# Large attention of a perceiver block: the scores for the row maximum from 64 rows of keys in two halves of the array, instead of from 128 rows

## The chip, the cores and the metric

The kernel runs as one program on one core of a Trainium2 chip (trn2). The metric is the time of one execution on the device in microseconds (us). The core has five engines that run side by side: TensorE (PE in the profile, its weight loads as PEld), VectorE (DVE), ScalarE (ACT), GpSimd (POOL) and SyncE (SP), which here only starts DMA transfers. They wait for one another by semaphores.

## What is computed

Two blocks of a perceiver, six sublayers with residuals, on x of shape (32, 64, 256) and a context of shape (32, 1601, 64). The change lies in the fourth sublayer, the large attention over the context, 16 heads:

```python
q_hk = (hidden_q @ Wq.T).reshape(Bv, Sv, H, K)
q_big = jnp.einsum('bshk,hkq->bshq', q_hk, w_kc_q)
q_big = _apply_rope(q_big, sin_q[None, :, None, :], cos_q[None, :, None, :])
kv_r = _apply_rope(kv_c, sin_k[None], cos_k[None])
q_r = jnp.einsum('bshq,hqr->bhsr', q_big, W_qr)
k_r = jnp.einsum('bld,hdr->bhlr', kv_r, W_kr)
scores = jnp.einsum('bhsr,bhlr->bhsl', q_r, k_r)
attn = jax.nn.softmax(scores, axis=-1)
ctx_c = jnp.einsum('bhsl,bld->bhsd', attn, kv_r)
ctx_lat = jnp.einsum('bhsd,hkd->bhsk', ctx_c, w_kc_kv)
```

In the kernel the products with the weights of queries and keys are merged, so that the scores are products of 64-element effective queries with the turned context.

## The kernel before

The phases run one after the other: three small attentions and two MLPs stand around the large attention (`context_attention`), which takes about 742 to 2519 us of the profiled execution. A batch there is one of the 32 sequences: 16 heads x 64 queries (1024 columns of queries) against 1601 keys in 13 tiles of 128 (the last has 65).

Numbers are kept as two parts in a reduced format (F32R), a high part and the rest. `kp` holds a batch's turned keys: the high parts in rows 0 to 63, the low parts in rows 64 to 127. `q1` holds the high parts of the queries in both halves of the rows. SyncE copies `kp` into `k1` and the high rows into `k2` (`move`), once a batch; `k2` and `q2` carry the rest of the product and the negated maximum in one further row.

For each tile kt of a batch n TensorE runs three thirds: `scores` for the first and for the second half of the heads (two 512-column products each, L813 and L814), and `values` (L825), which multiplies the exponentials that ScalarE made of an earlier tile. `values` writes to 64 of the 128 output rows at a time, so its products are 128 by 64 in the array, the others 128 by 128. GpSimd adds the exponentials up (L685).

The softmax needs each row's maximum ahead of the exponentials. So while batch n goes through its tiles, the maximum of batch n+1 is made in 16 pieces (`max_scores`, L790). A piece takes 128 query columns as weights and streams half of the keys as two products of 402 keys, into the two banks of one of the two `mx` buffers; VectorE reduces both banks in one instruction (`reduce_max`, L1062). Piece i waits for the reduction of piece i - 2. `pieces` sets where they stand: in an even batch (e = 0) from the second third of tile 1 to the second third of tile 6, in an odd one from tile 3 to tile 9, at most one behind each third. By that rule an even batch has 5 pieces behind the first scores of a tile, 6 behind the second scores and 5 behind the values; an odd batch has 6, 5 and 5. The 16 pieces of batch 0 stand side by side ahead of the first batch. Even batches also make the queries of the next two batches (L747, L761) in tiles 7 to 11.

The keys of batch n+2 are turned by TensorE in tiles 7 to 10 of batch n (L728) and kept in `kp` by ScalarE one tile later (L924).

Of the kernel before, what the change touches and what calls it, by code (L numbers as in the profile page):

```python
# [8 lines left out]
F32 = mybir.dt.float32  # L9
F32R = mybir.dt.float32r  # L10
# [5 lines left out]
P = 128  # L16
# [9 lines left out]
DCX = 64  # L26
# [375 lines left out]
SKP = 1608  # L402
KQ = SKP // 4
NKT = -(-SK // P)
SKT = NKT * P
KROUNDS = 4
# [75 lines left out]
def context_attention(nc, sb, pb, sem, a, x_all, const, wbig, mw, wvo):  # L482
# [16 lines left out]
    kr = sb("cx_kr", [P, NKT, DCX])  # L499
    khl = sb("cx_khl", [P, NKT, 2, DCX])  # L500
    kp = [sb(f"cx_kp{i}", [P, SKT], F32R) for i in range(2)]
    k1 = [sb(f"cx_k1{i}", [P, SKP], F32R) for i in range(2)]
    k2 = [sb(f"cx_k2{i}", [P, SKP], F32R) for i in range(2)]
    kv = [sb(f"cx_kv{i}", [P, NKT, DCX]) for i in range(2)]
# [21 lines left out]
    mx = [pb(f"cx_mx{i}", [P, 2, 512]) for i in range(2)]  # L526
# [13 lines left out]
    s_kl = sem("cx_kl_kept")  # L540
    s_kt = sem("cx_keys_transposed")
    s_kp = sem("cx_turned_keys_kept")
    s_kd = [sem("cx_even_keys_moved"), sem("cx_odd_keys_moved")]
    s_kv = sem("cx_kv_kept")
    s_var = sem("cx_variance")
# [53 lines left out]
    def batches(engine, before, batch):  # L599


        before()
        batch(0, 0, 0, True, True, True)
        with engine.Fori(0, NT - 2) as t:
            batch(2 * t + 1, t, 1, True, True, True)
            batch(2 * t + 2, t + 1, 0, True, True, True)
        batch(B - 3, NT - 2, 1, True, True, False)
        batch(B - 2, NT - 1, 0, False, True, False)
        batch(B - 1, NT - 1, 1, False, False, False)

    def is_first(n):
        return isinstance(n, int) and n == 0

    with nc.Block() as block:

        @block.sync
        def _(sp):
            def fetch(n):
                sp.dma_start(ctx[:, :, :], a["cx_ctxN"][bass.ds(n, 1), :, :, :]).then_inc(s_ctx, 16)
                sp.dma_start(ctxr[:, :, :], a["cx_ctxrN"][bass.ds(n, 1), :, :, :]).then_inc(s_ctx, 16)  # L620

            def move(n, e):

                sp.wait_ge(s_kp, KROUNDS * (n + 1))
                if not isinstance(n, int) or n >= 2:

                    sp.wait_ge(s_st, (n - 1) * 2 * NKT)
                sp.dma_start(k1[e][:, :].bitcast(F32), kp[e][:, 0:SKP].bitcast(F32)).then_inc(s_kd[e], 16)
                sp.dma_start(k2[e][0:DCX, :].bitcast(F32), kp[e][0:DCX, 0:SKP].bitcast(F32)).then_inc(s_kd[e], 16)

            def before():
                fetch(0)
                sp.wait_ge(s_kr, 1)
                fetch(1)
                sp.wait_ge(s_set, 6)
                move(0, 0)
                sp.wait_ge(s_kr, 2)
                fetch(2)

            def batch(n, t, e, more, next, far):  # L640
                if next:
                    move(n + 1, 1 - e)
                if far:

                    sp.wait_ge(s_kr, n + 3)
                    fetch(n + 3)

            batches(sp, before, batch)

        @block.gpsimd  # L650
# [69 lines left out]
        def _(pe):  # L720
# [52 lines left out]
            def max_scores(t, n, e, i):  # L773
                b = i % 2
                if i == 0:

                    pe.wait_ge(s_kp, KROUNDS * (n + 1))
                    if e == 0:
                        pe.wait_ge(s_q1a, 2 * t + 2)
                        pe.wait_ge(s_q2a, 2 * t + 2)  # L780
                    else:
                        pe.wait_ge(s_q1b, t + 1)
                        pe.wait_ge(s_q2b, t + 1)
                if not (is_first(n) and i < 2):

                    pe.wait_ge(s_mr, n * PIECES + max(i - 1, 0))
                q = q1[e][:, :, :, :].rearrange("p e j s -> p (e j s)")[:, (i // 2) * P:(i // 2 + 1) * P]
                for h in range(2):
                    lo = (2 * b + h) * KQ
                    last = pe.matmul(mx[b][:, h, 0:KQ], q, kp[e][:, lo:lo + KQ], start=True, stop=True)  # L790
                last.then_inc(s_mx, 1)

            def max_rows(n, p):
# [54 lines left out]
            def before():  # L848
                pe.wait_ge(s_set, 6)
                pe.wait_ge(s_one, 1)  # L850
                for r in range(KROUNDS):
                    turn_keys(0, r)
                turn_x(0)
                for j in range(CP + 2):
                    queries(0, j)
                for i in range(PIECES):
                    max_scores(0, 0, 0, i)
                for r in range(KROUNDS):
                    turn_keys(1, r)
                max_rows(0, 0)  # L860
                max_rows(0, 1)
                scores(0, 0, 0, 0, 0)
                scores(0, 0, 0, 0, 1)
# [1026 lines left out]
```

## Time and profile before

| | us |
|---|---|
| median of the three timed runs | 3383.43 |
| lowest and highest of them | 3383.25 and 3397.73 |
| the profiled execution | 3396.48 |
| its span, first to last instruction | 3394.7 |
| TensorE busy in the span | 2916.8 (86%) |
| VectorE, ScalarE, GpSimd busy | 1579.7, 1260.5, 1232.9 |

The profile is of one execution. Times in it are microseconds from the start of the span unless marked ns. An engine is busy while it computes; the ends of matmuls are modelled, since they are pipelined, so durations of two neighbours overlap, and the distance of two starts tells what one really takes.

### The profile page before, as it was taken

Reading aid. Unit: us, or ns where it says so; the run is one execution under the profiler, and the core shown is the slowest. Engines: PE = TensorE matmul, PEld = TensorE weight load, DVE = VectorE, ACT = ScalarE, POOL = GpSimd, SP = SyncE. Lnnn points to the kernel's source line nnn. Section 1 sums busy time; section 2 is a strip of 40 time slices with the busy share of each in tenths; the row PEclk is TensorE's granted clock in tenths of the full one; section 3 lists DMA queues with packets and bytes.
Section 4 is the critical chain, followed back from the end, with each engine's and each line's share of the span. In section 5 each row is a group of like instructions: output and inputs, shape, how many; then the busy total and the mean of one; then the engine's idle time right before and its main releaser. Section 6 shows DMA issues by size and latency. Waiting matters only on the chain. (4 is left out here: it accounts for less than half of the span.)

```text
span 3394.7 us, 49700 instructions
## 1 busy us (share of the span) xinstructions
PE 2916.8 (86%) x17527; PEld 1787.8 (53%) x17528; DVE 1579.7 (47%) x2705; ACT 1260.5 (37%) x2514; POOL 1232.9 (36%) x656
## 2 busy tenths in 40 slices
PE   5867734659999999999999999999977789999998
PEld 3544422535545554555455554555434467777776
DVE  3444567533554455444544464445526643333232
ACT  3433412114344334433443344344424333333332
POOL 0000000035676567656765676557650000000000
PEclk9778866679999999999999999999988899999999
DMA  1000030011111011110111111111011000000000
GB/s 40 0 17 0 0 121 0 0 58 40 36 49 39 25 35 49 39 35 33 41 39 35 39 35 39 35 39 35 30 72 77 0 1 0 0 0 0 0 0 25
DMA packets 26434, 98.27 MB, mean 29 GB/s; under 512 B 3536, under 2 KB 8272, under 8 KB 24976
## 3 DMA queue, kind: packets, MB, share of 16 engines
q1 hardware_dynamic: 24720, 94.02, 8.4%
q10 hardware_dynamic: 1664, 3.58, 0.3%
q8 instruction: 32, 0.52, 0.1%
q14 instruction: 18, 0.15, 0.0%
HBM read 55.97 MB, written 2.10 MB: 17 GB/s over the span
## 5 line engine op out<-in xcount | busy, mean ns | idle before, releaser
L685 POOL TENSOR_TENSOR cx_acc<-cx_acc,cx_prob 128x1024 f32<-128x1024 f32 (+1 forms) x352 | 834.7, 2371 | 509.0 <-ACT cx_prob L965 501.5
L965 ACT ACTIVATE cx_prob<-cx_st 128x512 f32<-128x512 f32 (+1 forms) x832 | 477.5, 596 | 595.2 <-PE cx_st L814 577.5
L1062 DVE TENSOR_REDUCE cx_mhalf<-cx_mx 128x1 f32<-128x804 f32 x512 | 486.1, 988 | 219.2 <-PE cx_mx L790 219.1
L825 PE MATMUL cx_av<-cx_prob,cx_kv 128*64 128x512 f32 (+1 forms) x1664 | 456.8, 628 | 0.0
L813 PE MATMUL cx_st<-cx_q,cx_k 128*128 128x512 f32 (+1 forms) x832 | 369.0, 444 | 50.0 <-ACT cx_prob L965 49.4
L1528 PE MATMUL moe_gu<-moe_wgu,moe_xnT 128*128 128x352 f32 x1280 | 397.6, 462 | 0.0
L790 PE MATMUL cx_mx<-cx_kp,cx_q 128*128 128x402 f32 x1024 | 304.0, 380 | 62.6 <-DVE cx_mhalf L1062 59.2
L814 PE MATMUL cx_st<-cx_q,cx_k 128*128 128x512 f32 (+1 forms) x832 | 332.4, 400 | 0.0
L1528 PEld LDWEIGHTS moe_gu<-moe_wgu,moe_xnT 128*128 128x128 f32 x1280 | 241.5, 191 | 124.1 <-issue 6.2
L790 PEld LDWEIGHTS cx_mx<-cx_kp,cx_q 128*128 128x128 f32 x1024 | 174.7, 193 | 248.5 <-DVE cx_mhalf L1062 186.0
L1043 DVE TENSOR_TENSOR cx_turn<-cx_mx,cx_tab 128x384 f32<-128x384 f32 x256 | 130.9, 553 | 358.3 <-PE cx_mx L747 358.3
L1663 DVE SCALAR_TENSOR_TENSOR moe_hid<-moe_silu,moe_coef,moe_gu 128x176 f32<-128x176 f32 x320 | 127.0, 397 | 350.2 <-ACT moe_silu L1591 348.1
L813 PEld LDWEIGHTS cx_st<-cx_q,cx_k 128*128 128x128 f32 (+1 forms) x832 | 157.8, 190 | 204.2 <-ACT cx_prob L965 143.7
L1591 ACT ACTIVATE moe_silu<-moe_gu 128x176 f32<-128x176 f32 x320 | 101.6, 318 | 370.8 <-PE moe_gu L1528 370.8
L1493 POOL TENSOR_TENSOR moe_rstd<-moe_mv,minus_half 128x1 f32<-128x1 f32 x16 | 8.8, 549 | 614.2 <-DVE moe_mv L1628 614.2
L1551 PE MATMUL moe_acc<-moe_wd,moe_hidT 128*128 128x256 f32 (+1 forms) x896 | 216.1, 382 | 0.0
L747 PE MATMUL cx_mx<-cx_xnT,cx_wbig 128*128 128x128 f32 x1536 | 204.7, 283 | 0.5 <-ACT cx_xnT L928 0.5
L761 PE MATMUL cx_mx<-cx_turn,cx_mw 128*64 128x128 f32 (+1 forms) x2048 | 197.0, 296 | 0.0
L747 PEld LDWEIGHTS cx_mx<-cx_xnT,cx_wbig 128*128 128x128 f32 x1536 | 183.2, 192 | 25.0 <-issue 16.5
L924 ACT CAST cx_kp<-cx_misc 128x512 fp32r<-128x512 f32 (+1 forms) x128 | 64.8, 507 | 324.2 <-PE cx_misc L728 324.2
L1551 PEld LDWEIGHTS moe_acc<-moe_wd,moe_hidT 128*128 128x128 f32 (+1 forms) x896 | 160.2, 190 | 21.9 <-issue 5.3
L814 PEld LDWEIGHTS cx_st<-cx_q,cx_k 128*128 128x128 f32 (+1 forms) x832 | 156.8, 188 | 7.5
(209 smaller groups left out, 3701.3 us busy)
## 6 DMA issues: line engine op xcount, KB each, us to landing
cx_k<-cx_kp SPq DMA_DIRECT2D x32, 804.0 KB, 4.0
cx_ctx<-in_cx_ctxN SPq DMA_DIRECT2D x32, 416.0 KB, 3.2
cx_ctxr<-in_cx_ctxrN SPq DMA_DIRECT2D x32, 416.0 KB, 3.9
cx_k<-cx_kp SPq DMA_DIRECT2D x32, 402.0 KB, 5.2
moe_wgu<-in_moe_wgu SPq DMA_DIRECT2D x5, 1408.0 KB, 14.6
moe_wd<-in_moe_wd SPq DMA_DIRECT2D x4, 896.0 KB, 24.6
x_all<-in_x SPq DMA_DIRECT2D x1, 2048.0 KB, 4.2
cx_wq<-in_cx_wq SPq DMA_DIRECT2D x1, 2048.0 KB, 11.8
```

What stands on the lines that cost most here:

```text
L685: pool.tensor_tensor(acc[rows, :, :], sofar, prob[slot(kt)][rows, :, :], ALU.add).then_inc(s_acc, 1)
L747: last = pe.matmul(mx[j % 2][:, 0, tile * P:(tile + 1) * P], wbig[:, c, j, tile * P:(tile + 1) * P], xnT[:, c, :], start=(c == 0), stop=(c ...
L761: last = pe.matmul(mx[j // 4][DCX * e:DCX * e + DCX, 1, at:at + P], mw[rows, j, cs, tile, :], turn[j % 2][rows, cs, tile, :, :], start=(cs ...
L790: last = pe.matmul(mx[b][:, h, 0:KQ], q, kp[e][:, lo:lo + KQ], start=True, stop=True)
L813: pe.matmul(st[p][0:nk(kt), :], k1[e][:, keys], q1[e][:, p, :, :], start=True, stop=False)
L814: pe.matmul(st[p][0:nk(kt), :], k2[e][:, keys], q2[e][:, p, :, :], start=False, stop=True)\
L825: last = pe.matmul(av[DCX * p:DCX * p + DCX, :], kv[e][0:nk(kt), kt, :], prob[slot(kt)][0:nk(kt), p, :], start=(kt == 0), stop=(kt == NKT ...
L965: act.activation(prob[slot(kt)][rows, p, :], st[p][rows, :], ACT.Exp).then_inc(s_exp, 1)
L1043: last = dve.tensor_tensor(turn[j % 2][:, cs, :, :, :], q, tab[:, cs, :, :].unsqueeze(2).broadcast_to([P, 3, 2, S]), ALU.mult)
L1062: dve.tensor_reduce(mhalf[:, i // 2, i % 2:i % 2 + 1], mx[i % 2][:, :, 0:KQ], AX.XY, ALU.max)\
L1528: last = pe.matmul(gu[i][:, 0:2 * FE], xnT[g][:, c, :], wgu[:, e, c, :], start=(c == 0), stop=(c == DC - 1))
L1551: last = pe.matmul(acc[:, 0:D], hidT[q % 2][0:n, k % 4, :], wd[0:n, k, :], start=(k == 0), stop=(k == NFC - 1))
```

## The change

Three edits. The low parts of the keys are left out of the maximum: each of a piece's two products now has 64 rows instead of 128, the first in rows 0 to 63 with `kp`, the second in rows 64 to 127 with a new tile `kh2`. `kh2` gets a second copy of the high parts in its upper rows by a new DMA of SyncE for each batch (`double`), which stands behind the fetch of the context in a batch and ahead of `move` of the next. TensorE's wait in front of the first piece is now for this copy instead of for `kp`. The scores that go into the exponentials are made as before.

```diff
+    kh2 = [sb(f"cx_kh2{i}", [P, SKP], F32R) for i in range(2)]
...
+            def double(n, e):
+
+                sp.wait_ge(s_kp, KROUNDS * (n + 1))
+                sp.dma_start(kh2[e][DCX:P, :].bitcast(F32), kp[e][0:DCX, 0:SKP].bitcast(F32)).then_inc(s_k2[e], 16)
+
             def before():
                 fetch(0)
                 sp.wait_ge(s_kr, 1)
                 fetch(1)
                 sp.wait_ge(s_set, 6)
+                double(0, 0)
                 move(0, 0)
                 sp.wait_ge(s_kr, 2)
                 fetch(2)
+                double(1, 1)
...
                     sp.wait_ge(s_kr, n + 3)
                     fetch(n + 3)
+                if more:
+                    double(n + 2, e)
...
-                    pe.wait_ge(s_kp, KROUNDS * (n + 1))
+                    pe.wait_ge(s_k2[e], 16 * t + 16)
...
-                for h in range(2):
-                    lo = (2 * b + h) * KQ
-                    last = pe.matmul(mx[b][:, h, 0:KQ], q, kp[e][:, lo:lo + KQ], start=True, stop=True)
+                for h, k in enumerate((kp[e], kh2[e])):
+                    lo, rows = (2 * b + h) * KQ, slice(DCX * h, DCX * h + DCX)
+                    last = pe.matmul(mx[b][:, h, 0:KQ], q[rows, :], k[rows, lo:lo + KQ], start=True, stop=True)
```

The order of TensorE's instructions stays as it is. On TensorE, the first pieces of an even batch, before (L813 and L814 are scores, L825 values, L790 the piece):

```order
L813 MATMUL cx_st<-cx_q,cx_k 128x512
L814 MATMUL cx_st<-cx_q,cx_k 128x512
L790 MATMUL cx_mx<-cx_kp,cx_q 128x402 x2
L825 MATMUL cx_av<-cx_prob,cx_kv 64x512 x2
L790 MATMUL cx_mx<-cx_kp,cx_q 128x402 x2
```

And now (L824 and L825 are the scores, L836 the values, L801 the piece; cx_kh is `kh2`):

```order
L824 MATMUL cx_st<-cx_q,cx_k 128x512
L825 MATMUL cx_st<-cx_q,cx_k 128x512
L801 MATMUL cx_mx<-cx_kp,cx_q 128x402
L801 MATMUL cx_mx<-cx_kh,cx_q 128x402
L836 MATMUL cx_av<-cx_prob,cx_kv 64x512 x2
L801 MATMUL cx_mx<-cx_kp,cx_q 128x402
L801 MATMUL cx_mx<-cx_kh,cx_q 128x402
```

Each piece keeps its place, and its second product reads another tile (the sizes are of the outputs, which don't change).

On SyncE, one batch of the loop, before (L628 and L629 are `move`, L619 and L620 `fetch`):

```order
L627 ISA [waits cx_turned_keys_kept]
L628 DMA cx_k<-cx_kp 128x1608 [waits cx_scores]
L629 DMA cx_k<-cx_kp 64x1608
L645 REGISTER_ALU
L619 ISA [waits cx_keys_summed]
L619 DMA cx_ctx<-in_cx_ctxN 128x832
L620 DMA cx_ctxr<-in_cx_ctxrN 128x832
```

And now:

```order
L629 ISA [waits cx_turned_keys_kept]
L630 DMA cx_k<-cx_kp 128x1608 [waits cx_scores]
L631 DMA cx_k<-cx_kp 64x1608
L654 REGISTER_ALU
L621 ISA [waits cx_keys_summed]
L621 DMA cx_ctx<-in_cx_ctxN 128x832
L622 DMA cx_ctxr<-in_cx_ctxrN 128x832
L635 REGISTER_ALU
L636 DMA cx_kh<-cx_kp 64x1608 [waits cx_turned_keys_kept]
```

The new copy stands last in the batch, ahead of the next batch's `move`.

## Rows read from the trace of the kernel before

**Rows 1.** The page's head, its busy table and its clock line (40 slices).

```profile
span 3394.7 us, 49700 instructions
...
PE 2916.8 (86%) x17527; PEld 1787.8 (53%) x17528; DVE 1579.7 (47%) x2705; ACT 1260.5 (37%) x2514; POOL 1232.9 (36%) x656
...
PEclk9778866679999999999999999999988899999999
```

**Rows 2.** Table by stretch (length, busy per engine, granted clock): stage, odd batch, even batch.

```profile
742.00:2519.00 1777.00, 1645.71 (x9025) 921.97 (x9024) 873.84 (x1108) 738.27 (x1341) 1149.21 (x520) 0.98 0.11 36
1501.50:1543.20 41.70, 37.53 (x170) 19.08 (x169) 24.76 (x31) 24.08 (x48) 32.83 (x16) 1.00 0.13 38
1543.20:1611.50 68.30, 64.76 (x406) 38.72 (x405) 31.03 (x41) 22.24 (x38) 39.87 (x18) 1.00 0.11 35
```

**Rows 3.** The page's groups: busy us, mean ns, idle before and its releaser.

```profile
L1062 DVE TENSOR_REDUCE cx_mhalf<-cx_mx 128x1 f32<-128x804 f32 x512 | 486.1, 988 | 219.2 <-PE cx_mx L790 219.1
...
L813 PE MATMUL cx_st<-cx_q,cx_k 128*128 128x512 f32 (+1 forms) x832 | 369.0, 444 | 50.0 <-ACT cx_prob L965 49.4
...
L790 PE MATMUL cx_mx<-cx_kp,cx_q 128*128 128x402 f32 x1024 | 304.0, 380 | 62.6 <-DVE cx_mhalf L1062 59.2
```

**Rows 4.** Timeline of TensorE in an odd batch (start, length, idle before).

```profile
1515.46 0.53 PE L790 MATMUL cx_mx<-cx_kp,cx_q 128*128 128x402 f32 x2
1515.83 0.39 PE L813 MATMUL cx_st<-cx_q,cx_k 128*128 128x512 f32 x1
...
1516.29 0.53 PE L790 MATMUL cx_mx<-cx_kp,cx_q 128*128 128x402 f32 x2
1516.75 1.08 PE L825 MATMUL cx_av<-cx_prob,cx_kv 128*64 128x512 f32 x4
1517.76 0.64 PE L790 MATMUL cx_mx<-cx_kp,cx_q 128*128 128x402 f32 x2
1518.23 0.39 PE L813 MATMUL cx_st<-cx_q,cx_k 128*128 128x512 f32 x1
...
1522.78 0.64 PE L790 MATMUL cx_mx<-cx_kp,cx_q 128*128 128x402 f32 x2 [1.05 <-DVE cx_mhalf L1062]
...
1531.95 0.33 PE L728 MATMUL cx_misc<-ident,cx_khl 128*128 128x128 f32 x1 [0.35 <-POOL cx_khl L668]
```

**Rows 5.** Timeline of TensorE in a small attention, 64 by 64 products (L241).

```profile
2575.47 1.09 PE L241 MATMUL a_score<-a_kbd,a_qT 64*64 64x256 f32 x16
...
2576.50 0.60 PE L235 MATMUL a_score<-maskb,identb 128*128 128x512 bf16 x2
```

**Rows 6.** Timeline of TensorE in the first attention: 128 by 128, 64 by 128, 64 by 64.

```profile
43.41 1.03 PE L194 MATMUL a_front<-a_wq,a_xnT 128*128 128x256 f32 x4
...
44.37 0.70 PE L196 MATMUL a_front<-a_wk,a_ctxT 64*128 64x256 f32 x2
...
45.00 0.65 PE L207 MATMUL a_v<-a_wv,a_ctxT 64*64 64x128 f32 x8
```

**Rows 7.** Timeline of TensorE in an even batch: the pieces that waited longest.

```profile
1560.53 0.63 PE L790 MATMUL cx_mx<-cx_kp,cx_q 128*128 128x402 f32 x2 [0.87 <-DVE cx_mhalf L1062]
...
1565.63 0.64 PE L790 MATMUL cx_mx<-cx_kp,cx_q 128*128 128x402 f32 x2 [1.66 <-DVE cx_mhalf L1062]
```

**Rows 8.** Timeline: last keys kept, first piece after; DMA table: us from issue to landing.

```profile
1541.42 0.27 ACT L924 CAST cx_kp<-cx_misc 128x128 fp32r<-128x128 f32 x1 [0.50 <-PE cx_misc L728]
...
1551.54 0.53 PE L790 MATMUL cx_mx<-cx_kp,cx_q 128*128 128x402 f32 x2
...
cx_k<-cx_kp SPq DMA_DIRECT2D x32, 804.0 KB, 4.0
...
cx_k<-cx_kp SPq DMA_DIRECT2D x32, 402.0 KB, 5.2
```

**Rows 9.** Table by stretch around one fall of the granted clock.

```profile
1620.30:1623.70 3.40, 1.59 (x7) 0.49 (x6) 1.81 (x3) 3.34 (x7) 1.83 (x1) 1.00 0.00 0
1623.70:1627.10 3.40, 3.40 (x9) 1.08 (x8) 0.80 (x1) 1.21 (x3) 3.15 (x2) 0.50 0.00 0
```

More of the change, by code:

```diff
@@ L542, in context_attention @@
     s_kp = sem("cx_turned_keys_kept")
+    s_k2 = [sem("cx_even_kh_doubled"), sem("cx_odd_kh_doubled")]
     s_kd = [sem("cx_even_keys_moved"), sem("cx_odd_keys_moved")]
```

## The prediction

> **What bounds the kernel now.** I read the page's head, its table of engines and its clock line first [rows 1]: TensorE is busy for 86% of the span, and its granted clock stands at nine tenths or more in nearly all slices of the long middle part. The part that the change touches is the context attention, about 742 to 2519 us. The table by stretch gives TensorE 1645.7 of those 1777 us, GpSimd 1149.2, VectorE 873.8, ScalarE 738.3 [rows 2]. So TensorE sets the pace there, and what it loses lies in short waits. The same table for one odd batch (41.7 us wide) and the even batch behind it (68.3 us) leaves TensorE idle for 4.2 and 3.5 us [rows 2]. The groups of the page say what it waits for at the pieces of the maximum: 59.2 us in all, for VectorE's reduction of an earlier piece [rows 3]. VectorE takes 486.1 us of busy time for 512 pieces, 0.95 us each [rows 3], and no piece can start before the reduction that frees its buffer. So there are two regimes: stretches where VectorE paces the pieces, in which time of TensorE is free, and stretches where TensorE works without a gap, in which every tenth of a microsecond counts.
>
> **What the pieces cost now.** In TensorE's timeline I take the time from one group's start to the next group's start, since the ends are modelled. A piece between two scores takes 0.37 us (1515.46 to 1515.83), so one 402-column product takes 0.18 [rows 4]. A piece in front of the values takes 0.46 (1516.29 to 1516.75), and a piece behind them 0.47 (1517.76 to 1518.23) [rows 4]. The values are 128 by 64 products, everything else here is 128 by 128. So each time the shape of the array changes, about 0.10 us goes by before the new shape starts, and its first product is another 0.10 late, since its weights aren't loaded ahead: 0.20 us for a change into a shape with 128 columns.
>
> **Part 1, the products.** One product over 128 rows becomes one over 64 rows, twice, in opposite halves. Two questions decide: do the halves run at once, and does a 64 by 128 shape count as another shape than 128 by 128?
> Halves at once: in the small attention sixteen 64 by 64 products of 256 columns, in both row halves and two banks, take from 2575.47 to 2576.50, 1.03 us [rows 5]. One such pass takes 0.215 us (below), so sixteen in a row would take 3.4 us; they run four at a time. I take this for the new pair, although it has 128 columns and passes once: a piece streams 0.18 us where it streamed 0.37, a gain of 0.18.
> Change of shape: the first attention has just this step. Four 128 by 128 passes of 256 columns take 0.96 us (43.41 to 44.37), which is 0.215 each and 0.10 for leaving; then two 64 by 128 passes take 0.63 (44.37 to 45.00), where 2 x 0.215 is 0.43 [rows 6]. So 64 by 128 pays the full 0.20 us, though only the rows differ.
> Sum by place. A piece between scores and scores adds two changes: 0.40 - 0.18 = +0.22 us. A piece beside the values, or one between values and scores, adds one, since the other is paid already: 0.20 - 0.18 = +0.02. By the kernel's schedule of pieces an even batch has 5 of the first kind and 11 of the second, an odd batch 6 and 10. That is 1.32 and 1.52 us of TensorE time. 16 even and 15 odd batches carry pieces: 21.1 + 22.8 = **44 us**, the upper bound of this part.
> What of it is covered. In the even batch TensorE waits 0.87 us for VectorE before the eighth piece and 1.66 us before the eleventh [rows 7]. The ten pieces that stand ahead of the second wait (three of the dear kind) add 0.80 us, less than the 2.53 of both waits, so it vanishes. Six pieces follow, two of them dear: 0.44 + 0.08 = 0.52, and I take 0.45 because the pieces there are already stretched a little by the same waits. In the odd batch a wait of 1.05 us before the sixth piece swallows what the first five add (0.50), and 0.35 us before the turning of the keys, a wait for GpSimd, swallows a part of the rest [rows 4]. Left are about 1.0 - 0.35 = 0.7 us. 16 x 0.45 + 15 x 0.7 = 7.2 + 10.5 = **18 us**, which is my term. Its lower bound is 0: all of it might fall into waits (TensorE stands for another 49.4 us behind ScalarE's exponentials [rows 3]). The 16 pieces ahead of the first batch are paced by VectorE and stand side by side, so nothing changes there.
> The Trainium skill speaks against the change in the same direction: "TensorEngine Tiling (Array Packing)", Key Properties, says that changing the tiling mode, not merely the tile, drains the engine; its Theoretical Speedup table promises up to 2x for 64 rows. By the table alone a piece would be worth its 0.18 us; the trace agrees with the drain and prices it at 0.20.
>
> **Part 2, the third copy.** SyncE issues one more DMA in every batch, 402 KB, ahead of the two that fetch the keys for the scores. The copy starts when the last round of turned keys is kept (1541.42 + 0.27 = 1541.69) and the first piece that needs it starts at 1551.54, 9.85 us later [rows 8]; on other batches the distance is longer. The existing copy of that size lands 5.2 us after its issue, behind one of 804 KB [rows 8]. So it is hidden, with over 4 us to spare, behind the last scores of the batch and the first two steps of the next. The keys' own copies go about one issue later and aren't needed before the end of the following batch. What queues behind the new wait on SyncE is only the next batch's copy, which waits for the same event or a later one. TensorE's wait for the copy takes the place of the wait for the keys. Cost: 0; if the cover were gone, 16 or 31 times what it is late.
>
> **Part 3, the clock.** The granted clock of TensorE is 0.98 over the stage [rows 2], so about 0.02 x 1777 / 0.5 = 71 us run at the lower of the two levels, 1.2 GHz; part of that is the start of the stage. Where it falls inside, the rows show what came before: 1.59 us busy of 3.4, then 3.4 us at 0.50 [rows 9]. Such a stretch costs at most 1.7 us. The change makes TensorE stream 0.18 us less for each of 16 pieces a batch, and standing still for a change of shape isn't streaming. The even batch's two waits for VectorE [rows 7] become spots as thin as the one in rows 9. Bounds: 0, and a fall in every even batch, 16 x 1.7 = 27 us. I take eight more falls of about 1 us, since part of each lies in a wait: **+8 us**.
>
> **Sum.** 18 + 0 + 8 = 26 us. The profiled execution has a span of 3394.7 us [rows 1] inside 3396.48; it would come to about 3422. The median of the runs is 3383.43, 13 us below the profiled one (one of the timed three was 3397.73), and the same 26 us on it give **3410**.
>
> **Rivals.**
> (a) The added changes of shape fall into waits, and the clock holds: the sum is 0 to 12 us, about 3388. For it: the idle time that TensorE has in both kinds of batch. Against: the six or more pieces behind the last wait.
> (b) Faster: splitting the rows isn't a change of shape for this pair, and weights for one half load while the other works. Then 0.18 us is gained for each piece. VectorE keeps the gain ahead of its waits; behind them 6 pieces in an even batch and 9 in an odd one count (11, less two whose gain the wait of 0.35 us for GpSimd takes): 16 x 6 x 0.18 + 15 x 9 x 0.18 = 17 + 24 = 41 us at most, and I put 35: 3348. It decides as soon as a change costs less than 0.135 us: there are 21 to 22 added changes to 16 pieces, and 0.18 x 16 / 21.5 = 0.135. Against it stands rows 6. In favour is one statement of the Trainium skill, "TensorE: Matmul & The Clock Gate", Part 3 (The mechanism), that weights load beside running products just where the row group differs; in rows 6 it doesn't help, since the step is from all rows to half of them.
> (c) The halves don't run at once in this number format with 128 columns and one pass. Then the 0.18 comes back, on the path for 6 pieces in an even and about 11 in an odd batch: 17 + 30 = 47 us more, and less streaming is then no reason for the clock to fall: 3383 + 18 + 47 = 3448, up to 3383 + 44 + 93 = 3520. Against: rows 5.
> (d) The copy is late. It must take twice what its like takes [rows 8]; 3 us late in every even batch would give 3383 + 26 + 48 = 3457.
>
> **How the numbers follow.** Forecast 0.62 (3396 to 3428), (a) 0.20, (b) 0.06, (c) 0.08, (d) and the rest 0.04. The range takes in (a) and the upper bound of the two terms (44 + 17): 3384 to 3444. About 0.5% (17 us) is what a measurement of this kernel can tell from no change, so slower means over 3400: most of the forecast, all of (c) and (d), 0.66; within 0.5% is (a) and the low end of the forecast, 0.28; faster is (b), 0.06.
>
> **What would show it.** Right: in the timeline the two products of a piece start within 0.01 us of each other; a piece between scores takes about 0.6 us from start to start; the odd batch is longer by 0.7 us, the even one by less; no wait at the first piece for a DMA. Wrong: products 0.18 us apart (c); a piece of 0.2 us with the next scores on time (b); the granted clock of the stage under 0.96 would mean that I put the clock too low.

## The result, and the profile after

The changed kernel takes **3449.12 us** (median of 4 runs, 3441.92 to 3460.75), the kernel before 3384.62 beside it (median of 4, 3383.25 to 3397.73): a ratio of **1.0185, 95% interval 1.0154 to 1.0215**. It is slower, as forecast, but by 64.5 us instead of 26, and 5 us outside the range. The profiled executions differ by the same amount, 3460.75 against 3396.48.

The page's head, its table of engines, its clock line and the groups of the touched lines, of the kernel after (columns as in [rows 1] and [rows 3]):

```profile
span 3459.0 us, 49732 instructions
...
PE 2993.3 (87%) x17527; PEld 1707.7 (49%) x17528; DVE 1592.5 (46%) x2705; ACT 1259.7 (36%) x2514; POOL 1229.2 (36%) x656
...
PEclk9778866669999999999999999999998989999999
...
L1073 DVE TENSOR_REDUCE cx_mhalf<-cx_mx 128x1 f32<-128x804 f32 x512 | 497.1, 991 | 266.9 <-PE cx_mx L801 262.2
...
L824 PE MATMUL cx_st<-cx_q,cx_k 128*128 128x512 f32 (+1 forms) x832 | 405.6, 487 | 49.6 <-ACT cx_prob L976 49.0
...
L801 PE MATMUL cx_mx<-cx_kp,cx_q 64*128 64x402 f32 x512 | 244.5, 478 | 50.9 <-DVE cx_mhalf L1073 47.5
...
L801 PE MATMUL cx_mx<-cx_kh,cx_q 64*128 64x402 f32 x512 | 244.7, 478 | 0.0
```

Against [rows 1] and [rows 3]: the piece is now two groups of 64 by 128 products side by side, 0.478 us each; VectorE's reduction has kept its length (991 ns against 988); TensorE's waits for it have shrunk from 59.2 to 47.5 us; and the other products of TensorE have grown, L824 from 444 to 487 ns in the mean, although nothing was done to them. The clock line looks almost as before. At 40 slices of 86 us it can't show what follows.

The table by stretch, of the kernel after: the stage, one odd batch, and the even batch behind it (length, busy of PE, PEld, DVE, ACT, POOL, granted clock, DMA):

```profile
742.00:2580.00 1838.00, 1715.53 (x9035) 838.14 (x9033) 886.83 (x1109) 741.08 (x1348) 1145.08 (x520) 0.95 0.14 41
...
1534.60:1579.10 44.50, 40.21 (x171) 16.16 (x167) 27.17 (x31) 24.73 (x46) 36.51 (x17) 0.96 0.20 56
1579.10:1650.70 71.60, 68.95 (x413) 37.46 (x415) 29.48 (x40) 22.00 (x41) 35.98 (x16) 0.95 0.12 35
```

The stage has 61 us more than in [rows 2], so nearly all of the loss is in it. From here on a batch is measured from the start of its predecessor's denominators to the start of its own; these are the products that sum up the exponentials (L837, now L848). Without a fall of the clock the kernel before has odd batches of 42.33 us and even ones of 68.2, two such batches of its own by the same table:

```profile
1507.20:1549.50 42.30, 37.77 (x171) 18.94 (x167) 26.77 (x31) 24.68 (x46) 36.62 (x17) 1.00 0.15 49
1549.50:1617.70 68.20, 65.02 (x411) 39.27 (x413) 29.01 (x40) 21.94 (x41) 36.07 (x16) 1.00 0.10 31
```

An odd batch in which the clock falls once takes 43.9 us there. After the change the first of the 14 full odd batches takes 43.0 and the others 44.5, and all 14 full even ones take 71.54 (the first batch of the stage and the last three, which stand without one part or another of the loop, aren't counted).

**Where the 3.3 us of an even batch go.** TensorE's timeline of the kernel after: two scores in a row, a piece between two scores, and the eleventh piece of an even batch:

```profile
1558.00 0.39 PE L825 MATMUL cx_st<-cx_q,cx_k 128*128 128x512 f32 x1
1558.23 0.39 PE L824 MATMUL cx_st<-cx_q,cx_k 128*128 128x512 f32 x1
...
1561.83 0.40 PE L825 MATMUL cx_st<-cx_q,cx_k 128*128 128x512 f32 x1
1562.15 0.44 PE L801 MATMUL cx_mx<-cx_kp,cx_q 64*128 64x402 f32 x1
1562.15 0.44 PE L801 MATMUL cx_mx<-cx_kh,cx_q 64*128 64x402 f32 x1
1562.53 0.51 PE L824 MATMUL cx_st<-cx_q,cx_k 128*128 128x512 f32 x1
1562.87 0.40 PE L825 MATMUL cx_st<-cx_q,cx_k 128*128 128x512 f32 x1
...
1592.64 1.08 PE L836 MATMUL cx_av<-cx_prob,cx_kv 128*64 128x512 f32 x4
1595.27 0.44 PE L801 MATMUL cx_mx<-cx_kp,cx_q 64*128 64x402 f32 x1 [1.55 <-DVE cx_mhalf L1073]
...
1595.66 0.63 PE L824 MATMUL cx_st<-cx_q,cx_k 128*128 128x512 f32 x1
...
1599.06 1.97 PE L836 MATMUL cx_av<-cx_prob,cx_kv 128*64 128x512 f32 x4
```

The two halves start together. Two scores in a row stand 0.23 us apart. From the score in front of the piece to the piece it is 0.32, from the piece to the next score 0.38, and from that to the one behind it 0.34: the changes of shape cost about what the prediction says. From the score in front of the piece to the second score behind it, the steps add up to 1.04 us; in the kernel before the same three steps around the piece at 1515.46 ([rows 4]) take 0.84, from the first to the second of these lines:

```profile
1515.22 0.40 PE L814 MATMUL cx_st<-cx_q,cx_k 128*128 128x512 f32 x1
...
1516.06 0.40 PE L814 MATMUL cx_st<-cx_q,cx_k 128*128 128x512 f32 x1
```

So a piece of this kind costs 0.20 us more, where the prediction has 0.22. But behind the wait of 1.55 us the values take 1.97 us where they took 1.08. The table by stretch around that wait, of the kernel after, and around the same wait of the kernel before ([rows 7], 1565.63):

```profile
1592.40:1595.80 3.40, 1.85 (x9) 0.58 (x10) 3.37 (x4) 0.57 (x1) 3.25 (x2) 1.00 0.36 89
1595.90:1599.30 3.40, 3.40 (x10) 1.40 (x11) 2.24 (x4) 1.36 (x3) 0.00 (x0) 0.50 0.39 149
1599.30:1602.70 3.40, 3.40 (x9) 1.27 (x8) 1.86 (x2) 0.60 (x1) 2.35 (x1) 0.50 0.00 0
1602.70:1606.10 3.40, 3.40 (x17) 2.80 (x15) 0.00 (x1) 0.00 (x0) 0.00 (x0) 1.00 0.00 0
...
1562.30:1565.70 3.40, 1.74 (x8) 0.57 (x7) 3.37 (x4) 0.69 (x2) 3.36 (x2) 1.00 0.35 88
1565.70:1569.10 3.40, 3.40 (x15) 1.86 (x15) 3.40 (x4) 1.97 (x3) 0.59 (x1) 1.00 0.42 163
```

TensorE is busy for 1.85 of 3.4 us, and then runs for 6.8 us at 0.50, its lower level of 1.2 GHz: 9 and 10 products in 3.4 us where 17 follow in the next. In the kernel before the same place is as thin (1.74 of 3.4), and the clock holds. Behind 850 us the clock's record of the kernel after has 28 such stretches with 143.4 us in them: one of 6.8 us in each of 14 even batches, always 16.7 to 16.8 us behind the batch's start, and one of 3.4 us in each of 14 odd ones (13 full ones and the one behind them). The kernel before has 10 stretches of 3.4 us there, 34.1 us in all, 9 of them in odd batches; an eleventh stands at 842 us, in its first odd batch. The granted clock over the whole span is 0.912 to 0.918 in all four runs of the changed kernel (0.928 in the profiled execution of the kernel before), so the profiled execution is no exception.

So the working theory behind the result: the added changes of shape cost some 15 us, and the clock the rest, nearly all of it in even batches. The rivals are that the even batches are longer through something else beside it (the copy, the halves' way through the array), and, for the clock, that the thin place alone decides.

### The profile page after: what moved, and what is told of

Same layout as the page of the kernel before. It is cut to its first block and busy times, and to the rows that moved or that the text cites. A ratio compares the mean times of both kernels' runs of the same rounds, so it can differ in the third digit from the quotient of the medians.

```text
span 3459.0 us, 49732 instructions
## 1 busy us (share of the span) xinstructions
PE 2993.3 (87%) x17527; PEld 1707.7 (49%) x17528; DVE 1592.5 (46%) x2705; ACT 1259.7 (36%) x2514; POOL 1229.2 (36%) x656
## 3 DMA queue, kind: packets, MB, share of 16 engines
q1 hardware_dynamic: 27280, 107.20, 10.2%
## 5 line engine op out<-in xcount | busy, mean ns | idle before, releaser
L1073 DVE TENSOR_REDUCE cx_mhalf<-cx_mx 128x1 f32<-128x804 f32 x512 | 497.1, 991 | 266.9 <-PE cx_mx L801 262.2
L836 PE MATMUL cx_av<-cx_prob,cx_kv 128*64 128x512 f32 (+1 forms) x1664 | 473.7, 649 | 0.0
L824 PE MATMUL cx_st<-cx_q,cx_k 128*128 128x512 f32 (+1 forms) x832 | 405.6, 487 | 49.6 <-ACT cx_prob L976 49.0
L825 PE MATMUL cx_st<-cx_q,cx_k 128*128 128x512 f32 (+1 forms) x832 | 338.5, 407 | 0.0
L801 PE MATMUL cx_mx<-cx_kp,cx_q 64*128 64x402 f32 x512 | 244.5, 478 | 50.9 <-DVE cx_mhalf L1073 47.5
L824 PEld LDWEIGHTS cx_st<-cx_q,cx_k 128*128 128x128 f32 (+1 forms) x832 | 157.6, 189 | 264.6 <-ACT cx_prob L976 138.4
L801 PEld LDWEIGHTS cx_mx<-cx_kp,cx_q 64*128 64x128 f32 x512 | 100.9, 197 | 333.8 <-issue 169.4
L801 PE MATMUL cx_mx<-cx_kh,cx_q 64*128 64x402 f32 x512 | 244.7, 478 | 0.0
```

What stands on the lines that cost most here:

```text
L801: last = pe.matmul(mx[b][:, h, 0:KQ], q[rows, :], k[rows, lo:lo + KQ], start=True, stop=True)
L824: pe.matmul(st[p][0:nk(kt), :], k1[e][:, keys], q1[e][:, p, :, :], start=True, stop=False)
L825: pe.matmul(st[p][0:nk(kt), :], k2[e][:, keys], q2[e][:, p, :, :], start=False, stop=True)\
L836: last = pe.matmul(av[DCX * p:DCX * p + DCX, :], kv[e][0:nk(kt), kt, :], prob[slot(kt)][0:nk(kt), p, :], start=(kt == 0), stop=(kt == NKT ...
L1073: dve.tensor_reduce(mhalf[:, i // 2, i % 2:i % 2 + 1], mx[i % 2][:, :, 0:KQ], AX.XY, ALU.max)\
```

## The experiments

Each ratio is against the kernel before on the same chip. "Clean" is a batch without a fall of the clock, and "hit" is one with it. A pair is an odd batch and the even one behind it, a thin place one where TensorE is busy for only half of some 3.4 us, and the dear pieces are those between two scores.

**The copy alone.** The changed kernel with the products as they were:

```diff
-                for h, k in enumerate((kp[e], kh2[e])):
-                    lo, rows = (2 * b + h) * KQ, slice(DCX * h, DCX * h + DCX)
-                    last = pe.matmul(mx[b][:, h, 0:KQ], q[rows, :], k[rows, lo:lo + KQ], start=True, stop=True)
+                for h in range(2):
+                    lo = (2 * b + h) * KQ
+                    last = pe.matmul(mx[b][:, h, 0:KQ], q, kp[e][:, lo:lo + KQ], start=True, stop=True)
```

> The third copy and the wait for it as in the changed kernel, the products as before (128 rows, from the keys' tile). Clock theory (the 64 us are about 18 us of changes of shape and over 40 us of lower clock) and shape theory (the waits cover far less than I thought, and the changes of shape are nearly all of it) both say: as before, 3376 to 3394. If the copy or its wait costs, the time goes towards 3449.

Measured: 3389.1 us, ratio 1.0001 (0.9982 to 1.0019). Clean batches of 42.35 and 68.26 us, 10 falls. In the DMA table of the kernel after the new copy lands 4.1 us after its issue, and the two copies of the keys now take longer (6.2 and 6.9, against 4.0 and 5.2 before, [rows 8]):

```profile
cx_k<-cx_kp SPq DMA_DIRECT2D x32, 804.0 KB, 6.2
...
cx_kh<-cx_kp SPq DMA_DIRECT2D x32, 402.0 KB, 4.1
cx_k<-cx_kp SPq DMA_DIRECT2D x32, 402.0 KB, 6.9
```

Part 2 holds: the new traffic and the moved wait cost nothing that can be told (the clean batches are 0.02 and 0.06 us longer).

**The halves in turn.** The changed kernel with both products in rows 0 to 63 of `kp`:

```diff
-                    last = pe.matmul(mx[b][:, h, 0:KQ], q[rows, :], k[rows, lo:lo + KQ], start=True, stop=True)
+                    last = pe.matmul(mx[b][:, h, 0:KQ], q[0:DCX, :], kp[e][0:DCX, lo:lo + KQ], start=True, stop=True)
```

> The changed kernel with both 64-row products of a piece in rows 0 to 63, so that they follow one another: all changes of shape are there, and the streaming takes as long as in the kernel before. The changes of shape then cost 0.40 or 0.20 us a piece with nothing gained: 4.2 us an even and 4.4 us an odd batch, of which about 1.7 and 3.0 are behind the last waits, 27 + 45 = 72 us. Clock theory: no more falls of the clock than before (stage at 0.98), so 3384 + 72 = 3456 within 12. If the clock goes by the rows in use instead of by the time that streams, it falls as well: stage at 0.95 or less and 3490 or more. Shape theory: 3500 or more at a clock of 0.98.

Measured: 3464.63 us, ratio 1.0227 (1.0184 to 1.0271). A piece between scores now takes 0.56 us where it took 0.38, in its timeline:

```profile
1540.90 0.40 PE L825 MATMUL cx_st<-cx_q,cx_k 128*128 128x512 f32 x1
1541.23 0.63 PE L801 MATMUL cx_mx<-cx_kp,cx_q 64*128 64x402 f32 x2
1541.79 0.50 PE L824 MATMUL cx_st<-cx_q,cx_k 128*128 128x512 f32 x1
```

Clean batches are 44.41 and 70.81 us; the clock falls in only 3 of 14 full even batches (75.47 us then, with 10.2 us at half). This is what rival (c) would have looked like: longer batches, with the clock at 0.99 between 850 and 2400 us, where the changed kernel has 0.96. The price of (c), 3448 and more, is just what the changed kernel measures, and the time alone would have spoken for the wrong rival. The two starts 0.01 us apart rule it out.

**Fewer columns.** The kernel before, where 200 columns of a product stand for 402, so half of the keys are left out of the maximum:

```diff
+                w = KQ if is_first(n) else 200
...
-                    last = pe.matmul(mx[b][:, h, 0:KQ], q, kp[e][:, lo:lo + KQ], start=True, stop=True)
+                    last = pe.matmul(mx[b][:, h, 0:w], q, kp[e][:, lo:lo + w], start=True, stop=True)
```

> The kernel before, but each of a piece's two products streams 200 columns instead of 402 (from the second batch on), so the maximum is taken over stale scores for the other half of the keys: this part of the computation is left out. VectorE still reduces 804 elements. The streaming is as thin as in the changed kernel, without any change of shape. Clock theory: the granted clock of the stage falls to about 0.95 and two stretches at 1.2 GHz stand in each pair of batches, as in the changed kernel; the even batch is near 71.5 - 1.5 = 70 us and the gain of shorter pieces (up to 41 us) is given back, 3365 to 3395. Shape theory: the clock stays at 0.98, and the time falls by 30 to 41 us, 3343 to 3354.

Measured: 3361.85 us, ratio 0.9922 (0.9895 to 0.9948), clean batches of 41.9 and 67.08 us, 11 falls with 41.0 us. A piece streams as briefly as after the change, without a change of shape. I had expected the clock of the stage to fall to about 0.95; between 850 and 2400 us it is 0.99, as in the kernel before. So streaming less doesn't by itself make the clock fall in batch after batch. It isn't ruled out as a part of the cause, since the batches have another length here as well, and the runs below show that the length counts.

**Something to do in the wait.** The changed kernel with a pair of products of zero weights (the trace records them as four) behind the values of one key tile of the even batch (`kt` 4), just ahead of the eleventh piece, where TensorE waits anyway; they add zero to the open sums:

```diff
+FILL = ((0, 4),)
...
+                            if (e, kt) in FILL:
+                                for p in range(2):
+                                    pe.matmul(av[DCX * p:DCX * p + DCX, :], zeros[:, :],
+                                              wvo[:, 0:2, :], start=False, stop=False)
```

> The changed kernel with one more pair of 512-column products (weights of zero, added to the values, shape of the values) behind the values of tile 4 in each even batch, in the wait of 1.5 us for VectorE after which the clock falls in every even batch. Clock theory: these falls go away, even batches drop from 71.5 to about 68.6 us, the time by 40 to 45 us to about 3406. Shape theory: nothing is gained, 3449 or a few us more.

Measured: **3406.15 us**, ratio 1.0050 (1.0023 to 1.0078). Work was added, and 43 us are gone. Its timeline at the place, and the table of an odd and an even batch:

```profile
1566.24 1.03 PE L885 MATMUL cx_av<-cx_wvo,cx_zeros 128*64 128x512 f32 x4
...
1567.96 0.45 PE L803 MATMUL cx_mx<-cx_kp,cx_q 64*128 64x402 f32 x1 [0.69 <-DVE cx_mhalf L1079]
...
1507.30:1551.80 44.50, 40.18 (x171) 16.17 (x168) 27.18 (x31) 24.77 (x46) 36.48 (x17) 0.96 0.20 56
1551.80:1620.30 68.50, 66.73 (x415) 36.68 (x417) 29.31 (x40) 21.93 (x41) 36.00 (x16) 1.00 0.13 36
```

The wait of 1.55 us is 0.69 now, the even batches stand at 68.52 with a clock of 1.00, and only odd batches still fall, 10 of them as before. 71.54 - 68.52 is 3.02 us for the double stretch, 14 times 42 us. What is left, 68.52 - 68.2 in even and 43.0 - 42.33 in odd batches, is the price of the changes of shape, less what the shorter streaming gives back.

**The same filler elsewhere.** `FILL = ((0, 9),)`: the thin place stays as it was, and the batch is 0.9 us longer.

> The changed kernel with the same extra pair of products, but behind the values of tile 9 of each even batch, where TensorE never waits, instead of in the thin place at tile 4. Thin-place theory: the falls of the clock at tile 4 stay in every even batch, and the pair costs its own 0.9 us on top: 3449 + 14 = 3463 within 12. Lock theory (any change of the batches' length breaks the pattern in which each even batch is hit, and the place of the extra pair doesn't matter): most falls go, 3410 to 3430.

Measured: 3411.43 us, ratio 1.0088 (1.0058 to 1.0118). Two even batches of this kernel by the table by stretch, one clean and one hit:

```profile
1322.30:1391.70 69.40, 66.77 (x417) 36.68 (x419) 29.31 (x40) 21.95 (x41) 35.99 (x16) 1.00 0.12 36
...
1547.10:1619.40 72.30, 69.67 (x415) 37.70 (x417) 29.48 (x40) 21.90 (x41) 35.97 (x16) 0.95 0.12 35
```

Only 3 of 14 full even batches are hit, though the waits are as they were. This is the wait ahead of the eleventh piece in the clean batch, busy for 1.85 us of 3.4 as in the changed kernel, and the stretch behind it:

```profile
1335.10:1338.50 3.40, 1.85 (x10) 0.43 (x8) 3.37 (x4) 0.73 (x2) 3.40 (x2) 1.00 0.20 32
1338.50:1341.90 3.40, 3.40 (x14) 1.30 (x14) 3.40 (x4) 1.85 (x3) 0.74 (x2) 1.00 0.55 218
```

The theory that the thin place alone decides falls with this run. What it shows instead is that the length of the loop counts. In the changed kernel a pair of batches with its falls takes 71.54 + 44.53 = 116.07 us, and its falls stand 116.05 us apart (899.5 to 2408.2 us, 13 pairs): each comes at the same point of its batch. In the kernel before a hit pair takes 43.88 + 68.2 = 112.1 us, and neighbouring falls stand 112.6 us apart (954.7 and 1067.3; 1289.2 and 1401.9): each comes half a microsecond later in its batch, 6.3 us behind the start, then 6.9, and after two or three of them the next odd batch is missed. In the run above a hit pair takes 43.0 + 72.3 = 115.3 us (117.0 where the stretch lasts 10.2 us), and no two neighbours are hit. I call this the rhythm theory: the same thin place is hit again in the next pair if the pair, with its falls, lasts about as long as the distance at which falls repeat, 116.05 us in the one kernel and 112.6 in the other. What sets these distances, no run shows.

**Whole products for the dear pieces.** Pieces between two scores go back to 128 rows, so that no change of shape stands beside them; the others stay split:

```diff
-                for h, k in enumerate((kp[e], kh2[e])):
-                    lo, rows = (2 * b + h) * KQ, slice(DCX * h, DCX * h + DCX)
+                for h, k in enumerate((kp[e], kp[e] if whole else kh2[e])):
+                    lo, rows = (2 * b + h) * KQ, slice(0, P) if whole else slice(DCX * h, DCX * h + DCX)
```

> The changed kernel with the pieces between scores and scores (5 of 16 in an even, 6 in an odd batch) as whole-row products as before; the other 10 or 11 stay in two halves. By my sum of the changes of shape only 0.02 us a piece is left: even batch 68.2 to 68.4, odd batch 42.3 without a fall. Clock: the place ahead of the eleventh piece is filled with one product more than in the changed kernel, so I expect few falls there or none: 3384 to 3396. If the falls of the even batches stay, 3425 to 3435.

Measured: 3388.05 us, ratio 1.0000 (0.9982 to 1.0019). Clean batches of 42.07 and 68.0 us, shorter than those of the kernel before by 0.26 and 0.2; 12 falls with 44.4 us: 9 of 14 full even batches are hit, eight of them with single stretches, where the kernel before has one, and 3 odd ones. I had expected few falls or none, so the clock's part is a miss, and so are the clean batches, which are shorter than expected. The dear pieces are the whole price of the change of shape. What the cheap ones gain, 16 x 0.2 + 15 x 0.26 = 7 us, is more than half kept in the trace (1675.9 us from the first denominators to the last, against 1679.9), the rest going to the falls; the ratio of the runs is too coarse for it.

**Filled on both sides.** The kernel before with the filler in the odd batch, `FILL = ((1, 1),)`, and the changed kernel with both, `FILL = ((0, 4), (1, 1))`:

> The kernel before with the extra pair of products (weights of zero, added to the values) behind the values of tile 1 in each odd batch, where TensorE waits 1.8 us for ScalarE and where ten falls of the clock stand in the trace of before. Clock theory: these falls go away, each was worth 1.55 us: 15 us less than before, ratio 0.9955. If what falls there isn't a matter of the thin place: no change or up to 14 us more.

> The changed kernel with the extra pair at both thin places (tile 4 of even and tile 1 of odd batches). What is left against the kernel before is then the changes of shape alone (0.35 us an even and 0.67 us an odd batch in the trace of the run filled at tile 4, 16 us in all) less the 15 us of the falls that the kernel before still has: 3384 to 3392. Without an effect of the second place: 3406.

Measured: **3368.59 us**, ratio **0.9936** (0.9916 to 0.9956), and 3391.05 us, ratio 1.0006 (0.9989 to 1.0022). Of the second, an even and an odd batch, and 1550 us of the stage:

```profile
1537.30:1605.90 68.60, 66.78 (x417) 36.70 (x419) 29.32 (x40) 22.06 (x41) 36.00 (x16) 1.00 0.12 36
1605.90:1648.90 43.00, 39.55 (x175) 16.03 (x171) 27.19 (x31) 24.73 (x46) 36.56 (x17) 1.00 0.20 58
...
850.00:2400.00 1550.00, 1477.76 (x8190) 734.38 (x8192) 781.61 (x985) 649.97 (x1183) 1004.55 (x457) 1.00 0.15 45
```

No fall is left behind 850 us in the changed kernel, and one in the filled kernel before, whose batches stand at 42.32 and 68.2. The two differ by 22.5 us in the medians, by 14 us in the traces from the first denominators on (1678.2 against 1664.6 us to the last). The 14 us are the change with the clock nearly taken out of it (15 without the one fall); the other 8.5 of the medians aren't explained, with runs of the first kernel between 3381.6 and 3398.1. And the kernel before had room of its own: of its eleven falls the ten in odd batches are gone, 1.55 us each, which is 15.5 of the 23 us between its median and that of its filled version. The rest of these isn't explained either.

**Twice the filler elsewhere, and late in the odd batch.** On the changed kernel `FILL = ((0, 9), (0, 10))` and `FILL = ((1, 9),)`, to make the pair still longer in two ways:

> The changed kernel with two extra pairs of products, behind the values of tiles 9 and 10 of each even batch, far from the thin place at tile 4. Rhythm theory (the thin place falls only where it meets the clock's own rhythm, and in the changed kernel two batches with their falls last just as long as it takes to meet it again, 116.07 us every time): the pair of batches gets another length, falls at tile 4 come in some even batches and not in all. Without falls it would be 3391 + 16 x 1.8 = 3420, with some 3420 to 3440. Place theory (the place alone decides): all falls stay, 3449 + 28 = 3477.

> The changed kernel with one extra pair behind the values of tile 9 of each odd batch, after its last piece. Rhythm theory: as in the run with the pair at tile 9 of the even batches, 3405 to 3425, with falls at tile 4 in fewer than 8 of 15 even batches. Place theory: 3449 + 14 = 3463.

Measured: 3456.4 us, ratio 1.0196 (1.0162 to 1.0230), and 3426.19 us, ratio 1.0106 (1.0082 to 1.0129). The first is a miss: 16 falls with 102.4 us, 11 of 14 full even batches hit, not the few that a longer pair was meant to leave; the time lies between what the two theories gave (3440 at most and 3477). Its batches offer an account, found after the result. A clean pair takes 43.0 + 70.2 = 113.2 us, but with its fall 43.0 + 73.2 = 116.2, and its falls stand 116.0 to 116.1 us apart (1000.6, 1116.6, 1232.7, 1348.7). If it is the length with the fall that counts, this kernel is back near the 116.05 us of the changed one. The second hits 4 of 14 full even batches, as expected, at a time 1 us above the range given; its pairs take 43.2 + 73.5 = 116.7 us with their fall, and no two neighbours are hit.

**A shifted start.** The changed kernel without a filler in the loop (`FILL = ()`), with four products of zero weights once ahead of it:

```diff
+                for f in range(4):
+                    pe.matmul(av[DCX * (f % 2):DCX * (f % 2) + DCX, :], zeros[:, :], wvo[:, 0:2, :], start=True, stop=True)
```

> The changed kernel with two extra pairs of products once, ahead of the first batch: the loop starts 1.8 us later and nothing in it differs. Rhythm theory: the pattern draws itself in again after the first batches, since a pair with its falls lasts 116.07 us whatever the start was; 28 falls within 3, 3449 within 12. If the start decided, the falls would be far fewer, 3400 to 3420.

Measured: 3450.29 us, ratio 1.0167 (1.0146 to 1.0189), 26 falls with 133.1 us. The table by stretch of its first full even batch, the odd one behind it, the next even one, and the 6.8 us in that:

```profile
880.30:948.80 68.50, 65.87 (x413) 36.40 (x415) 29.32 (x40) 21.95 (x40) 35.97 (x16) 1.00 0.13 38
948.80:991.80 43.00, 38.68 (x173) 15.78 (x169) 27.18 (x31) 24.75 (x46) 36.54 (x17) 1.00 0.21 58
991.80:1063.30 71.50, 68.86 (x413) 37.46 (x415) 29.48 (x40) 21.95 (x40) 35.98 (x16) 0.95 0.12 35
...
1008.60:1012.00 3.40, 3.40 (x10) 1.37 (x10) 2.32 (x4) 1.52 (x3) 0.08 (x1) 0.50 0.33 130
1012.00:1015.40 3.40, 3.40 (x9) 1.37 (x6) 1.71 (x2) 0.45 (x1) 2.27 (x1) 0.50 0.00 0
```

One even batch comes through clean, at 68.5; in the next the clock falls 16.8 us behind its start, and then in every one, at the same point as in the changed kernel. So the hits don't hang on this one start. The clean batch at 68.5 us, without a filler in it, also shows that the filler at tile 4 adds nothing to the length of a batch.

**Both remedies.** Whole products for the dear pieces and both fillers:

> Candidate for a faster version: pieces between scores as whole-row products, the others in two halves, and the extra pair of products at both thin places (tile 4 of even, tile 1 of odd batches). Clean batches of 42.1 and 68.0 us, as in the run with whole dear pieces, against 42.3 and 68.2 us in the kernel before, and no falls: 15 x 0.45 = 7 us under the kernel before filled at tile 1, 3362, ratio 0.9915.

Measured: 3370.74 us, ratio 0.9930 (0.9910 to 0.9950); batches of 42.11 and 68.0, no fall. I had expected 3362 and 0.9915. It beats the kernel before, but by its runs not the filled kernel before (0.9936, whose interval overlaps; between the denominators the trace is 7.8 us shorter, 1656.8 against 1664.6, and the medians don't show it), which needs neither the second copy of the keys nor the split.

## Why the prediction was wrong where it was

**Part 1, the changes of shape: right.** A score in front of a piece is 0.09 us longer than one in front of a score (0.32 against 0.23), the one behind it 0.11 (0.34), and the piece takes 0.38. By the clean batches the change costs 0.32 us in an even batch (68.52 - 68.2; 0.45 predicted) and 0.7 in an odd one (43.0 - 42.33; 0.7 predicted), 16 x 0.32 + 15 x 0.7 = 16 us for 18. The upper bound of 44 us was far off, since the waits do swallow most. One sign was put wrongly: the step from the piece to the next score is 0.38 us and not "about 0.6 us", since the price of 0.20 stands ahead of the piece and in the score behind it. The run with whole products for the dear pieces undoes the price with them. The Trainium skill, "TensorEngine Tiling (Array Packing)", Key Properties, says that changing the tiling mode drains the engine; this trace agrees, with 0.09 us ahead of the new shape, here for a change of rows alone.

**Part 2, the copy: right.** Cost 0, measured alone at a ratio of 1.0001. The last keys are kept at 1570.97 + 0.27 = 1571.24 us and the first piece starts at 1581.25, 10 us later, for a copy that lands in 4.1.

**Part 3, the clock: the step that failed.** "I take eight more falls of about 1 us", with an upper bound of 16 x 1.7 = 27. Behind 850 us there are 18 more falls, and 109 us more at 1.2 GHz. Priced by batches: 14 even ones of 71.54 instead of 68.52 are 42 us, less 1.4 for the one even batch that fell before; and four more odd ones that fell (14 for 10), at 1.5 us each, are 6. That makes some 47 us for 8. Filling the waits gives it back: 43 us less with the even batches filled. Three things were wrong:
- the reason. I wrote that the two waits of the even batch would "become spots as thin as the one in rows 9". The second was that thin already, 1.74 us busy of 3.4, and the clock held there. With half the columns the kernel before had 11 falls for 10. Whether a thin place is hit isn't decided by how thin it is alone.
- the number. I took eight, half of the bound of one in every even batch, and gave no reason for the half; more falls in odd batches I didn't count at all. All 14 full even batches are hit: the pair with its falls takes 116.07 us and the falls stand 116.05 us apart, through the whole stage.
- the size. I priced a fall at the 3.4 us stretch of rows 9. The one in the even batch lasts 6.8 us and costs 3.0, where the bound was 1.7.

The range had a slip besides: it took 17 us as the upper bound of this part, where the part itself says 27. With 27 it would have ended at 3454, above the measured time, and the clock would have been mis-sized all the same, at 47.

The sum from what was measured: 15 to 16 us for the shapes and 47 for the clock are 62 or 63, for 64.3 between the profiled executions. The rest is at the start of the stage, where the first denominators come between 822 and 840 us in all kernels alike, with no order that belongs to the change.

**The rivals.** (a) fell: the clock didn't hold. On its other half the runs are less clear: with the falls left as they were before, in the kernel filled in its even batches, the change costs 14.5 us by the medians, where (a) allowed 0 to 12, but the interval of that ratio reaches down to 8 us; the clean batches say 15 to 16. (b) fell: a change of shape costs more than the 0.135 us from which the split would pay. Where it has none of the dear kind, the batches are indeed shorter, by 0.2 us. (c) had the right time for a wrong reason (its upper end is 3516 by its own 0.18 us a piece, not 3520). (d) fell with the copy alone. Of the signs of being right, the two products of a piece within 0.01 us, 0.7 us more in an odd batch and less in an even one (both clean), and no wait for a DMA at the first piece came in. Of the signs of being wrong, "the granted clock of the stage under 0.96 would mean that I put the clock too low" did, at 0.95.

**Open.** Why a low stretch lasts 6.8 us behind the even batch's wait (10.2 at times, when the half rows go in turn or a filler stands elsewhere) and 3.4 us behind the odd one's, isn't shown. Nor is the rule by which one thin place is hit and its equal isn't. That hit pairs repeat at 116.05 to 116.1 us and at 112.6 us is measured, and that the length with the fall decides fits three kernels that are hit on and on (the changed one, the shifted start, twice the filler) and three that aren't (the filler elsewhere, late in the odd batch, halves in turn: 115.3, 116.7 and 119.9 us); but for twice the filler it was found only afterwards, 116.7 lies close to 116.2 and is hit only now and then, and with the halves in turn the place ahead of the falls is fuller too (2.39 us busy of 3.4). The kernel with whole dear pieces fits neither group: its hit pairs take 111.6 us, or 113.1 with a fall in the odd batch, its neighbouring falls stand 112.6 us apart, and 9 of 14 even batches are hit. No run gave the kernel before pairs as long as the changed one's with its shapes as they are, which would tell what the length does by itself from what the changes of shape beside the wait do.

## What to carry to other kernels

A loop in which TensorE waits at one place can lose clock there, and the mean busy share doesn't show it. So before a change to such a loop is judged, list the falls of the clock batch by batch, and compare with a version in which the clock holds. A cheap way to such a version is a product with zero weights into an open sum, where TensorE waits anyway; on the kernel before it is worth 0.64% by itself. And count the changes of array shape that a split by rows adds at each place: where a change stands there anyway, the split pays here (batches shorter by 0.2 us); between two products of one shape it costs 0.20 us a piece more than 402 columns give back.

## What the runs showed of the hardware

- Two 64 by 128 products of 402 columns in opposite row halves, each with weights of its own, start 0.01 us apart and together take the time of one (0.38 us from the piece to the next score, against 0.56 in turn).
- Whether the clock falls behind a wait isn't settled by the wait alone: with TensorE busy for 1.85 of the 3.4 us around it, 14 of 14 even batches were hit where a hit pair lasts 116.07 us, 3 at 115.3, 4 at 116.7, 11 at 116.2, and 13 of 14 after a shifted start.
- A stretch at 1.2 GHz was 3.4, 6.8 or 10.2 us long, and cost 1.55, 3.0 and 4.65 us of a batch (43.88 - 42.33, 71.54 - 68.52, 75.47 - 70.81).
- Products with zero weights hold the clock up: 143 us at the lower level behind 850 us become none.
